# Expert gate weights as rows loaded from DRAM instead of products on TensorE, and a third bank for the products under silu

## What is computed

```python
logits = xt @ w_gate
top_logits, sel = jax.lax.top_k(logits, TOP_K)          # TOP_K = 2 of 8
probs = jax.nn.softmax(top_logits, axis=-1)
h = jax.nn.silu(einsum('td,edh->eth', xt, w1)) * einsum('td,edh->eth', xt, w3)
y = einsum('eth,ehd->etd', h, w2)
out = sum over the two chosen experts of probs * y
```

## Time and profile before

| | us |
|---|---|
| three runs | 2752.12, 2752.49, 2756.4 |
| median | 2752.49 |
| span of the profiled execution | 2757.4 |
| PE busy in it | 2492.9 (90%) |
| DVE busy | 1977.2 (72%) |
| ACT busy | 1522.7 (55%) |
| POOL busy | 1484.2 (54%) |
| moe0, its first DMA to that of the layer after, first time | 453.5 to 662.0 |
| moe1, the same, first time | 1573.3 to 1901.3 |

### The profile page before, as it was taken

One profiled execution on the slowest core, in us unless ns is written; L12 is line 12 of the kernel. 1 busy time (PEld: TensorE's weight loads), 2 busy tenths in 40 slices (PEclk: granted clock), 3 DMA queues, 4 the chain that ended last, 5 costly groups with the idle time before them and its releaser, 6 DMA issues. The chain is left out here.

```text
span 2757.4 us, 40750 instructions
## 1 busy us (share of the span) xinstructions
PE 2492.9 (90%) x12972; PEld 1587.4 (58%) x12972; DVE 1977.2 (72%) x4522; ACT 1522.7 (55%) x2424; POOL 1484.2 (54%) x1371
## 2 busy tenths in 40 slices
PE   4477998998789989989999899998999999979999
PEld 3344565666756566644444478776444444357877
DVE  6865776775667667756666588887777778668887
ACT  4632454444435544446666456654677677656665
POOL 5924654443265544356666555654766566335554
PEclk8787899998969999989999999999999999889999
DMA  1001110000021000010000100000000000010000
GB/s 47 0 3 29 36 34 25 1 1 19 1 49 39 13 26 1 1 56 1 1 1 1 45 1 1 1 1 16 1 1 1 1 0 1 1 43 9 8 5 12
DMA packets 38561, 36.73 MB, mean 13 GB/s; under 512 B 12888, under 2 KB 28120, under 8 KB 38104
## 3 DMA queue, kind: packets, MB, share of 16 engines
q1 hardware_dynamic: 38360, 34.26, 4.6%
HBM read 19.42 MB, written 2.10 MB: 8 GB/s over the span
## 5 line engine op out<-in xcount | busy, mean ns | idle before, releaser
L2328 DVE TENSOR_REDUCE l_diffneg_max<-psum 128x1 fp32r<-128x512 f32 x512 | 335.7, 685 | 96.6 <-PE psum L2066 92.3
L4475 POOL TENSOR_TENSOR l_moe1sc<-l_moe1s,l_moe1bcs 128x512 f32<-128x512 f32 x192 | 266.3, 1394 | 235.8 <-ACT l_moe1s L4284 197.7
L2243 ACT ACTIVATE l_diffweights<-psum 128x1024 f32<-128x1024 f32 x256 | 261.9, 1025 | 138.3 <-PE psum L2095 137.4
L2066 PE MATMUL psum<-l_diffkz,l_diffQ 128*128 128x512 f32 (+1 forms) x512 | 238.3, 484 | 2.9 <-DVE l_diffneg_max L2328 2.0
L4373 DVE TENSOR_TENSOR x<-l_moe1sc,psum 128x512 f32<-128x512 f32 x256 | 174.4, 681 | 92.8 <-POOL l_moe1sc L4475 82.0
L2868 ACT ACTIVATE l_lightswapped<-psum 32x512 f32<-32x512 f32 x304 | 179.0, 589 | 100.8 <-DVE l_lightturned L2960 97.4
L4380 DVE TENSOR_TENSOR l_moe1g_lo<-x,l_moe1g_hi 128x512 fp32r<-128x512 f32 x256 | 224.5, 878 | 1.1 <-ACT l_moe1g_hi L4263 1.1
L4284 ACT ACTIVATE l_moe1s<-psum 128x512 f32<-128x512 f32 x256 | 153.3, 600 | 100.8 <-PE psum L852 93.7
L1592 DVE TENSOR_REDUCE l_attn0neg_max<-psum 128x1 fp32r<-128x512 f32 x256 | 167.3, 683 | 54.5 <-PE psum L1326 51.8
L173 POOL TENSOR_TENSOR settled<-powers 128x1 f32<-128x1 f32 x111 | 35.2, 317 | 305.9 <-DVE l_alibimv L699 73.5
L1498 ACT ACTIVATE l_attn0weights<-psum 128x1024 f32<-128x1024 f32 x128 | 130.2, 1023 | 121.7 <-PE psum L1348 121.7
(11 more groups left out here) (603 smaller groups left out, 7096.0 us busy)
## 6 DMA issues: line engine op xcount, KB each, us to landing
l_attn0Q<-l_attn0q_hi SPq DMA_DIRECT2D x128, 64.0 KB, 2.0
l_moe1w_raw<-in_moe_w SPq DMA_DIRECT2D x20, 256.0 KB, 5.5
l_attn0Q<-l_attn0q_lo SPq DMA_DIRECT2D x64, 64.0 KB, 2.0
l_moe0w_raw<-in_moe_w SPq DMA_DIRECT2D x20, 128.0 KB, 2.5
x<-in_x SPq DMA_DIRECT2D x8, 256.0 KB, 4.9
out<-x SPq DMA_DIRECT2D x8, 256.0 KB, 2.3
open_raw<-in_moe_w SPq DMA_DIRECT2D x8, 128.0 KB
l_attn0Q<-l_attn0max_rows SPq DMA_DIRECT2D x64, 2.0 KB, 1.7
```

The costliest lines, as they stand in the source:

```text
L2066: nc.tensor.matmul(ps[:, bank, :], Q[rows, n % 4, st * P:(st + 1) * P], kz[rows, n % 4, hh, :], start=True, stop=True).then_inc(pe_max.sem ...
L2243: nc.scalar.activation(weights[:, tt, 2 * pair:2 * pair + 2, :], ps[:, S[m % 2]:S[m % 2] + 2, :], ACT.Exp, scale=SCALE).then_inc(act_exp.s ...
L2328: nc.vector.tensor_reduce(neg_max[:, n % 2, st, row:row + 1], ps[:, bank_of(("max", n, b)), :], AXX, ALU.max, negate=True).then_inc(vec_ma ...
L4475: nc.gpsimd.tensor_tensor(sc[:, n % 2, h, :], s[:, n % 2, h, :], bcs[:, n % 2, :], ALU.mult).then_inc(pool_sc.sem, pool_sc.step("sc", h))
```

## The change

The gate weights are no longer spread by TensorE. ScalarE writes the transposed weights in full precision to open_rows (`rows_out`), SP stores the 8 rows of 512 to a DRAM tensor `gate_rows` (`store_rows`, 16 KB), waits until they are there, and loads each expert's row back into all 128 partitions of a place of bcs (`spread_rows`, 256 KB written). bcs has six places. The scaling waits on the semaphore of the place (`row_ready`). The row products, their bank's copies, `pick`, `rows_low` and the second copy of comb are gone. The transposes of comb move in moe0 from slot 8 to slot 7. Bank 7 becomes the third of H1, and TensorE waits for the silu of three products back instead of two. For the first sequence the layer ahead stores the rows and waits for it at the end of its SP stream (`rows_kept`), and the mixture's SP stream loads rows 0 to 5 between the weight groups.

```diff
@@ class Gate
-    def rows_high(self, a, j, bank):
+    def rows_out(self, a, j, bank):
         of = self.act_comb
         of.start()
+        if j > self.begins:
+            a.wait_ge(self.rows_stored, 16 * (j - self.begins))
         a.wait_ge(self.pe_comb.sem, self.pe_comb.done(j, "comb"))
-        self.core.nc.scalar.activation(self.rows(j), self.core.psum[:, bank, :], ACT.Copy).then_inc(of.sem, of.step("hi"))
+        self.core.nc.scalar.activation(self.core.open_rows[:, :], self.core.psum[:, bank, :], ACT.Copy).then_inc(of.sem, of.step("rows"))
...
-        inc(v.tensor_tensor(self.comb[:, :, 0:8], self.hot1[:, :, :], self.hot2[:, :, :], ALU.add), "comb", 0)
-        inc(v.tensor_tensor(self.comb[:, :, LO_ROW:LO_ROW + 8], self.hot1[:, :, :], self.hot2[:, :, :], ALU.add), "comb", 1)
-
-    def rows_low(self, d, j, bank):
...
+    def store_rows(self, sp, j):
+        sp.wait_ge(self.act_comb.sem, self.act_comb.done(j, "rows"))
+        sp.dma_start(self.core.dram["gate_rows"][j], self.core.open_rows[0:8, :]).then_inc(self.rows_stored, 16)
@@ class Opening
+    def rows_kept(self, sp):
+        self.gate.store_rows(sp, 0)
+        sp.wait_ge(self.gate.rows_stored, 16)
@@ moe_block
-    H1, H3, OUT, MISC, BC = (0, 1), (2, 3, 4), 5, 6, 7
+    H1, H3, OUT, MISC = (0, 1, 7), (2, 3, 4), 5, 6
...
-    AT_CHOICE, AT_E2, AT_WEIGHTS, AT_COMB = (4, 4, 5, 8) if moe.shared else (2, 2, 3, 5)
+    AT_CHOICE, AT_E2, AT_WEIGHTS, AT_COMB = (4, 4, 5, 7) if moe.shared else (2, 2, 3, 5)
...
+    ROWS = 6
...
-        bcs = sb("bcs", [P, 2, T])
+        bcs = sb("bcs", [P, ROWS, T])
...
+            def spread_rows(j, experts):
+                for e in experts:
+                    n = j * NE + moe.shared + e
+                    k = rowed(n)
+                    if k >= ROWS:
+                        j_, e_ = divmod(k - ROWS, moe.experts)
+                        for h in range(HT):
+                            scaling_done(sp, j_ * NE + e_ + moe.shared, h)
+                    sp.dma_start(weights_row(n), core.dram["gate_rows"][j, e, :].unsqueeze(0).to_broadcast([P, T])
+                                 ).then_inc(row_loaded[k % ROWS], 16)
...
+            for g in range(weights_in.groups):
+                spread_rows(0, range(2 * g, min(2 * g + 2, ROWS)))
+                weights_in.sync_group(sp, g)
             if opening:
                 opening.sync_part(sp)
+            spread_rows(0, range(ROWS, moe.experts))
+            for j in range(1, NSEQ):
+                chooser.store_rows(sp, j)
+                sp.wait_ge(chooser.rows_stored, 16 * j)
+                spread_rows(j, range(moe.experts))
+                if store:
+                    tokens_out(j - 1)
...
-                    if u >= 2:
-                        t.wait_ge(act_silu.sem, act_silu.done((u - 2) // HT, "silu", (u - 2) % HT))
+                    if u >= 3:
+                        t.wait_ge(act_silu.sem, act_silu.done((u - 3) // HT, "silu", (u - 3) % HT))
...
-            def weight_rows(n):
...
-                nc.tensor.matmul(ps[:, BC, :], pick[:, e - moe.shared, :], comb_rows(j), start=True, stop=True
-                                 ).then_inc(pe_bc.sem, pe_bc.step("row"))
...
-                copy(bcs[:, n % 2, :], ps[:, BC, :]).then_inc(act_bc.sem, act_bc.step("row"))
```

More of the change, by code:

```diff
@@ L344, in __init__ @@
             comb = ctx.enter_context(core.nc.sbuf_tensor(f"l{n}_next_comb", [P, NQ, P], F32))
-            self.gate = Gate(core, ctx, f"l{n}_next", self.first.bias if layer == "moe0" else None, self.first.gate, comb,
-                             lambda j: core.open_rows[:, :])
+            self.gate = Gate(core, ctx, f"l{n}_next", self.first.bias if layer == "moe0" else None, self.first.gate, comb)
         self.counted, self.averaged = sem("statistics_vector"), sem("means_vector")
@@ L1230, in freed @@
             if what == "comb":
-                return opening.gate.vec_comb.sem, opening.gate.vec_comb.done(0, "lo")
+                return opening.gate.act_comb.sem, opening.gate.act_comb.done(0, "rows")
             if what == "max":
@@ L1665, in _ @@
                     normalise(s - 1)
-                if m == 4 and s == OPENS + 2:
-                    opening.gate.rows_low(d, 0, bank_of(("comb", 0)))
                 if m == 6 and s == OPENS:
@@ L2006, in _ @@
             opening.sync_part(sp)
+            opening.rows_kept(sp)
         @block.tensor
@@ L2408, in pair_of_sequences @@
                             opening.gate.weights(d, 0)
-                        if last and (G, m) == (7, 1):
-                            opening.gate.rows_low(d, 0, bank_of(("q", 10)))
             ident = core.ident[:, :].rearrange("p (h r) -> p h r", r=STRIP)
@@ L3066, in _ @@
             tail(NSEQ - 1)
-            opening.gate.rows_low(d, 0, EVEN)
         @block.gpsimd
@@ L4007, in operands, with sync_group @@
         return self.hi[:, base + c:base + c + P], self.lo[:, base + c:base + c + P]
-    def sync_part(self, sp):
-        for g in range(self.groups):
-            for _, at in self.columns(g):
-                sp.dma_start(self.raw[:, at], self.core.dram[self.source][:, at]).then_inc(self.loaded[g], 16)
+    def sync_group(self, sp, g):
+        for _, at in self.columns(g):
+            sp.dma_start(self.raw[:, at], self.core.dram[self.source][:, at]).then_inc(self.loaded[g], 16)
     def wait_loaded(self, engine, g):
@@ L4124, in misc_free @@
                     return
-                of, step = {"tail": (vec_tail, "tail"), "tr": (vec_lo, "lo"), "gate": (chooser.vec_gate, "logits"), "comb": (chooser.vec_comb, "lo")}[what]
+                of, step = {"tail": (vec_tail, "tail"), "tr": (vec_lo, "lo"), "gate": (chooser.vec_gate, "logits"), "comb": (chooser.act_comb, "rows")}[what]
                 t.wait_ge(of.sem, of.done(j, step))
@@ L4237, in _ @@
                 j, e = divmod(n, NE)
-                if EARLY <= n < N and not is_shared(n):
-                    weight_rows(n)
                 if real(n):
@@ L4245, in _ @@
                     tail(j - 1)
-                if n == EARLY - 1:
-                    for m in range(moe.shared, EARLY):
-                        weight_rows(m)
                 if turns(n) and j + 1 < NSEQ:
@@ L4268, in head_hi @@
                 copy(h_hi[:, j % 2, :], ps[:, MISC, :]).then_inc(act_hi.sem, act_hi.step("hi"))
-            def weight_rows(n):
-                act_bc.start()
-                if n >= 2:
-                    for h in range(HT):
-                        scaling_done(a, n - 2, h)
-                a.wait_ge(pe_bc.sem, pe_bc.done(rowed(n), "row"))
-                copy(bcs[:, n % 2, :], ps[:, BC, :]).then_inc(act_bc.sem, act_bc.step("row"))
             def silu(n, h):
```

96 lines of the change are left out of this document (41 added, 55 removed).

## The result

Before 2754.44 us, median of 4 runs (2752.12 to 2764.16); after 2730.69, median of 4 (2728.36 to 2731.68). The ratio is 0.9908, interval 0.9891 to 0.9926: 23.8 us faster, against 31 forecast; the range of 2700 to 2746 holds it.

The account below looks back on a forecast made before the run. TensorE was taken as the bound, clearly in moe0, narrowly in moe1, where VectorE bounds part of a sequence. Gains of 18.0 (moe0) and 13.4 us (moe1), less 0.5, gave 30.9 off 2752.5: 2722 us, range 2700 to 2746.

Parts of the forecast that it names:

- The row product: TensorE's slot of one expert in moe0: each removed row product frees 0.235 us, the slot going from 2.50 to 2.26 us.
- 21 of 64 in moe1 lost behind VectorE: Three row products in each of seven moe1 sequences lie where VectorE's queue sets the pace, so removing them gains nothing.
- The third bank: Third bank for h1 lifts TensorE's wait on an earlier silu; no such steady wait exists, so it gains nothing.
- Steady loads hidden: Row loads of 256 KB, 0.95 to 1.3 us each, fit within slots of 2.26 us (moe0) and 4.2 us (moe1).
- The first row: Each moe0 sequence's first row needs 5.2 us for store and load, with 5.4 us available; cost put at 0.
- moe0's start: Row loads ahead of weight group 2 make the gate products 3.6 us late; a lower clock costs 2.0 us more per layer.
- moe1's start: Row loads ahead of the weight groups make the gate products of each moe1 layer 2.9 us late.
- Light's end: At the end of light, a store of about 2.2 us follows ScalarE's copy and replaces VectorE's rows_low: +0.5 us.
- (a): Rival: the layer starts cost little, so about 50 us are gained, giving 2703 us; chance 0.22.
- (b): Rival: moe1 gains nothing per slot and moe0's first rows come late by 0.3 us on TensorE: 2745 us; chance 0.14.
- (c): Rival: loads do not keep up and set moe0's slot; at 4 us a load the kernel takes 2944 us; chance 0.05.
- (d): Rival: no change, since layer starts of 12 us each use up the 50 us gain: 2751 us; chance 0.04.

## Why the prediction was right

- **The row product, 0.235 us.** Right, to the hundredth: the slot went from 2.50 to 2.26 us, and putting the product back alone made it 2.50.
- **21 of 64 in moe1 lost behind VectorE.** Right for the sequences that took 36.93 us: 1.4 us less than 38.31, where 1.2 was forecast and the product put back costs 1.2. It missed the collision. With the change GpSimd's scaling went from 0.1 us behind VectorE's instruction to level with it or just ahead, and in half of the steady sequences VectorE lost about 1.1 us. The ten steady periods gave 0.81 us each on average, 3.7 us less in all than the 1.2 each of the forecast. This is the term of the sum that was mis-sized. The stretch behind the last gate products of a layer gave 3.4 and 3.0 us where the sum has 2.6, so that 2.4 us are missing over both layers. The rule of the Trainium skill (SBUF — State Buffer, "Who interferes with whom") that the prediction quoted was the right one, and it was put aside with "nothing in this change relieves it"; that a change can make it worse was not asked.
- **The third bank, 0.** Right.
- **Steady loads hidden.** Right, up to twice their number. The rule of the Trainium skill (SBUF — State Buffer, "SBUF: two separate sides"), that DMA writes and engine accesses do not contend, agrees: GpSimd's scaling takes 1.40 us with all loads going and no collision, 1.42 before with none.
- **The first row, needed 5.2 of 5.4 us.** Needed 4.65, and there were 5.78. The estimate by the fit in the Trainium skill (DMA: Bandwidth & Descriptors, "Anatomy of one DMA"), 4.6, was nearer than mine, although that section gives the fit for DMAs issued by GpSimd, and SP issues these. The conclusion held, but the cushion I named did not exist: a late row is felt within the slot, through head_lo, as the transposes a slot later showed. The one slot that the change moved them was needed.
- **moe0's start, 3.6 + 2.0 us.** The size was right, the place not: it was put on group 2, and group 1 was already late, with 1 MB of rows ahead. The rate of 250 GB/s "when going" was also read too low: the rows give 205 / 0.76 = 270 and 273 / 0.91 = 300, and by 270 the same sum makes the gate 2.8 us late, not 3.6; it was 4.15 and 3.25. From the first transfer to the second gate products it now takes 40.29 and 38.57 us against 34.97 and 36.02; with eight row products (1.9) that would have gone, the starts cost 7.2 and 4.4, 5.8 on average. That this average meets 5.6 is in part luck. In the first layer the granted clock fell as forecast (0.51 and then 0.70, against 1.00 and 1.00 before), in the second less (0.76 and 0.84, against 0.81 and 1.00).
- **moe1's start, 2.9 us.** The gate products are 2.8 and 2.0 late; by the same reckoning to the second gate products (62.87 and 63.36 against 59.83 and 62.92, where five row products gone would have given 1.2) the starts cost 4.2 and 1.6, 2.9 on average. The average is what was forecast, but neither layer is.
- **Light's end, +0.5.** It was +0.1: from the copy's end to the first transfer of moe1 takes 2.69 us with the store, 2.74 before with VectorE's rows_low in its place.
- **The sum.** 30.9 forecast; 27.5 in the profiles, 23.8 in the medians. Of the 3.4 between forecast and profile 2.4 are moe1's, 0.6 moe0's, and the rest other layers' (+0.8, unexplained, with the light's end better by 0.4). The medians differ by 3.7 us less than the profiled spans: the kernel before's span lies 3.0 us over its median, the changed kernel's 0.8 under.
- **The rivals.** (a), cheap starts, is refuted by the start distances; it becomes nearly true with the weights ahead of the rows (moe0's starts then cost 1.8 and 0.9 us by the reckoning above). (b) was half right on moe1, for another reason, and wrong on first rows. (c) and (d) were far off.

## What to carry to other kernels

A load that is free in the steady part is paid where the queue is already full: at a layer's start, put what an engine's queue waits for first, ahead of what is needed one slot later. When work is taken from the engine that is the bound, look at which instructions of other engines now meet, and read the two engines' timelines for the same microsecond; a collision can take back most of the gain in some repetitions and not in others. A result that is late costs not by who wants it, but by what is queued behind its consumer.
